# Moving small VectorE operations of a graph attention kernel to TensorE: own scores, both edge bounds and a constant one

## The reference

```python
h = x @ W                                      # 8192 x 128
e = (h @ a1)[:, None] + (h @ a2)[None, :]      # own score + neighbour's score
e = where(e > 0, e, 0.2 * e)                   # leaky slope
e = where(adj > 0, e, -9e15)
h_prime = softmax(e, axis=1) @ h
out = layernorm(x + elu(h_prime), eps=1e-5)    # over the 128 features
```

## Time and profile before

| what | us |
|---|---|
| median of 3 runs | 719.73 (718.51 to 720.04) |
| the profiled execution's own time | 722.26 |
| span of its profile | 720.5 |
| TensorE busy | 558.7 |
| VectorE busy | 482.4 |
| ScalarE busy | 520.8 |
| GpSimd busy | 440.6 |

### The profile page before, as it was taken

The page is one execution under the profiler, slowest core; times in us unless marked ns, Lnnn a source line. Parts: engine busy times, 40 slices in busy tenths (PEclk is TensorE's granted clock), DMA queues, the critical chain, the costliest instruction groups (busy, mean ns, idle before and its releaser), DMA issues.

```text
span 720.5 us, 11885 instructions
## 1 busy us (share of the span) xinstructions
PE 558.7 (78%) x3023; PEld 356.0 (49%) x3071; DVE 482.4 (67%) x2059; ACT 520.8 (72%) x414; POOL 440.6 (61%) x668
## 2 busy tenths in 40 slices
PE   0867887777777888787777988877777888787794
PEld 0333455444455555555445655554455555554483
DVE  1376677785766667777776567777766667776754
ACT  0847777777887878787887778787877878777410
POOL 2015457766766676767666576667766676776731
PEclk9978999997999988999998788999999988998955
DMA  8999999999999999999999999999999999999062
GB/s 351 328 417 429 425 421 428 428 423 425 427 428 426 427 428 426 425 429 425 427 429 426 428 425 428 426 429 428 425 425 430 428 426 428 425 426 407 24 171 80
DMA packets 34582, 285.57 MB, mean 396 GB/s; under 512 B 5512, under 2 KB 13856, under 8 KB 18048
## 3 DMA queue, kind: packets, MB, share of 16 engines
q1 hardware_dynamic: 29008, 276.83, 91.9%
q0 software_dynamic: 5120, 8.42, 3.3%
q10 hardware_dynamic: 432, 0.07, 0.1%
HBM read 283.18 MB, written 4.19 MB: 399 GB/s over the span
## 4 chain that ended last, share of the span: by engine, by line
DMA 71%; ACT 11%; PE 10%; issue 5%; DVE 2%; SPq 1%; ACTq 0%; POOLq 0%; POOL 0%; DVEq 0%
DMA adj_sb<-in_adj 68%; ACT adj_squared L558 10%; PE fold L660 5%; DMA a_sb<-in_L_gnn_a 2%; PE x_att_ps L713 1%; PE misc L685 1%; PE small L694 1%; PE fold L656 1%; SPq L402 1%; PE fold L757 1%; PE small L675 1%; PE x_att_ps L716 0%; DVE spread L376 0%; DVE stats L1000 0%; DVE x_sb L996 0%
## 5 line engine op out<-in xcount | busy, mean ns | idle before, releaser
L558 ACT ACTIVATE adj_squared<-adj_sb 128x4096 bf16<-128x4096 int32 x128 | 462.6, 3614 | 114.3 <-DMA adj_sb<-in_adj 111.7
L660 PE MATMUL fold<-adj_sb,bit_ident 128*128 128x512 bf16 x993 | 301.7, 448 | 9.1 <-DMA adj_sb<-in_adj 3.8
L503 POOL DMA_INDIRECT nb<-in_x,index x160 | 165.1, 1032 | 94.7 <-issue 68.7
L660 PEld LDWEIGHTS fold<-adj_sb,bit_ident 128*128 128x128 bf16 x1024 | 110.0, 107 | 151.6 <-issue 63.1
L868 DVE MAX8 top_map<-fold 128x8 f32<-128x512 f32 x128 | 89.5, 699 | 69.2 <-PE fold L660 64.3
L656 PE MATMUL fold<-col_no,ident_bf 128*128 128x512 bf16 x112 | 46.7, 417 | 111.3 <-DMA adj_sb<-in_adj 104.0
L364 POOL TENSOR_SCALAR edge_row<-row_iota,edge_in 128x128 f32<-128x128 int32 x186 | 128.1, 702 | 0.0
L382 POOL TENSOR_TENSOR spread<-edge_row,edge_w 128x384 f32<-128x384 f32 x60 | 54.4, 925 | 80.6 <-DVE edge_w L984 80.5
L656 PEld LDWEIGHTS fold<-col_no,ident_bf 128*128 128x128 bf16 x128 | 16.3, 127 | 131.8 <-issue 90.1
L483 POOL TENSOR_SCALAR empty_diag<-ident,counts 128x128 f32<-128x128 f32 x64 | 39.1, 616 | 59.6 <-DVE counts L904 32.7
L713 PEld LDWEIGHTS x_att_ps<-spread,nb 128*128 128x128 f32 x372 | 59.1, 226 | 9.2 <-issue 4.2
(11 more groups left out here) (120 smaller groups left out, 629.3 us busy)
## 6 DMA issues: line engine op xcount, KB each, us to landing
adj_sb<-in_adj SPq DMA_DIRECT2D x127, 2048.0 KB, 14.7
out<-x_sb SPq DMA_DIRECT2D x2, 1536.0 KB, 10.3
nb<-in_x,index POOLq DMA_INDIRECT x160, 2.4
adj_sb<-in_adj SPq DMA_DIRECT2D x2, 1024.0 KB, 16.1
out<-x_sb SPq DMA_DIRECT2D x5, 128.0 KB, 3.4
out<-x_sb SPq DMA_DIRECT2D x1, 384.0 KB, 10.0
W_sb<-in_L_gnn_W ACTq DMA_DIRECT2D x1, 64.0 KB, 7.8
x_sb<-in_x SPq DMA_DIRECT2D x4, 0.5 KB, 17.6
```

Source lines behind the costliest of these rows:

```text
L503: nc.gpsimd.indirect_dma_start(out=nb_of(j, g)[:, c, :], out_offset=None, in_=x[:, :], in_offset=bass.IndirectOffsetOnAxis(ap=index[:, g, ...
L558: nc.scalar.activation(adj_squared[:, h % 2, :], adj_sb[:, h % LOAD_SLOTS, :], ACT.Square, accum_out=half_sum[:, h:h + 1]).then_inc(square ...
L660: last = nc.tensor.matmul(fold[:, h % LOAD_SLOTS, :], bit_ident[:, b, :], adj_low[:, h % LOAD_SLOTS, b * FOLD:(b + 1) * FOLD, 0], start=Fa ...
```

## The change

TensorE makes four things that VectorE made, or makes them unneeded. A matmul with the identity puts the row's own score into `t_row_ps` ahead of the neighbours' scores (one matmul for each tile in `send_scores`). `count_starts` has a second matmul with a triangle that includes the diagonal, so it gives start and end of a row's edges at once, and `route` adds the base to both in one operation. `times_W` first adds a matmul of two rows of ones, so that PSUM holds h + 1; ScalarE takes off the one by a bias operand, and the minimum and the maximum of `finish` become one operation. `scores` takes the minimum with `cap` (whose low value is now NEG / ALPHA) ahead of the leaky slope. GpSimd keeps `found` and the ends by two copies in `tally` in place of one.

```diff
-        before = sb("before", [P, P], fp32)
+        before = sb("before", [P, 2, P], fp32)
-        starts_ps = misc[:, 160:160 + PAIR]
+        starts_ps = misc[:, 160:160 + 2 * PAIR].rearrange("p (t k) -> p t k", k=2)
...
-                    nc.gpsimd.tensor_copy(counts_all[:, :, tiles], counts[:]).then_inc(tallied, 1)
+                    nc.gpsimd.tensor_copy(found_all[:, tiles], found[:])
+                    nc.gpsimd.tensor_copy(ends_all[:, tiles], sent[:, :, END_COL]).then_inc(tallied, 1)
...
-                    nc.scalar.activation(z_exp[:, g, :, :], h_of(j, g)[:, :, 0:D], ACT.Exp).then_inc(elu_exp, 1)
+                    nc.scalar.activation(z_exp[:, g, :, :], h_of(j, g)[:, :, 0:D], ACT.Exp,
+                                         bias=minus_one[:, 0:1]).then_inc(elu_exp, 1)
...
-                    nc.tensor.matmul(starts_ps, before[:], found, start=True, stop=True).then_inc(starts_made, 1)
+                    for k in range(2):
+                        last = nc.tensor.matmul(starts_ps[:, :, k], before[:, k, :], found[:], start=True, stop=True)
+                    last.then_inc(starts_made, 1)
...
                     for t in range(PAIR):
+                        mine = s_all[:, bass.ds(j * BODY + g * PAIR + t, 1)]
+                        nc.tensor.matmul(t_row_ps[:, t, :], ident[:], mine.to_broadcast([P, SLOTS]),
+                                         start=True, stop=False)
                         for k, c in enumerate(SPANS[t]):
                             last = nc.tensor.matmul(t_row_ps[:, t, :], edge_row[:, g, t, k, :], t_slot[:, c, :],
-                                                    start=k == 0, stop=k == SPAN - 1)
+                                                    start=False, stop=k == SPAN - 1)
...
-                        last = nc.tensor.matmul(h_of(j, g)[:, t, 0:D], x_att[:, t, :], W_sb[:], start=True, stop=True)
+                        nc.tensor.matmul(h_of(j, g)[:, t, 0:D], ones[0:1, :], ones[0:1, :], start=True, stop=False)
+                        last = nc.tensor.matmul(h_of(j, g)[:, t, 0:D], x_att[:, t, :], W_sb[:], start=False, stop=True)
...
-                nc.vector.tensor_scalar(before[:], offset[:], 0.0, None, ALU.is_gt)
+                for k, compare in enumerate((ALU.is_gt, ALU.is_ge)):
+                    nc.vector.tensor_scalar(before[:, k, :], offset[:], 0.0, None, compare)
...
-                    v.after(nc.vector.tensor_tensor(sent[:, :, START_COL], starts_ps, tile_edge[:], ALU.add))
-                    v.after(nc.vector.tensor_tensor(ends, sent[:, :, START_COL], found, ALU.add))
+                    v.after(nc.vector.tensor_tensor(sent[:, :, START_COL:END_COL + 1], starts_ps,
+                                                    tile_edge[:].unsqueeze(2).to_broadcast([P, PAIR, 2]), ALU.add))
...
-                    v.after(nc.vector.tensor_tensor(score[:], t_row_ps, mine.unsqueeze(2).to_broadcast(slots),
-                                                    ALU.add))
-                    v.after(nc.vector.scalar_tensor_tensor(score_l[:], score[:], ALPHA, score[:],
-                                                           ALU.mult, ALU.max))
-                    v.after(nc.vector.tensor_tensor(score_l[:], score_l[:], cap[:, g, :, :], ALU.min))
+                    v.after(nc.vector.tensor_tensor(score[:], t_row_ps, cap[:, g, :, :], ALU.min))
+                    v.after(nc.vector.scalar_tensor_tensor(score_l[:], score[:], ALPHA, score[:], ALU.mult, ALU.max))
...
-                    v.after(nc.vector.tensor_scalar(z_one[:], z_exp[:, g, :, :], 1.0, None, ALU.min))
-                    nc.vector.scalar_tensor_tensor(elu[:], h_of(j, g)[:, :, 0:D], 1.0, z_one[:], ALU.add, ALU.max
+                    nc.vector.scalar_tensor_tensor(elu[:], z_exp[:, g, :, :], 1.0, h_of(j, g)[:, :, 0:D], ALU.min, ALU.max
```

More of the change, by code:

```diff
@@ L95, in graph_attention @@
     SENT = CODES + 2
-    ROW_COL, START_COL = CODES, CODES + 1
+    ROW_COL, START_COL, END_COL = CODES, CODES + 1, CODES + 2
     adj_tiles = adj.rearrange("(t p) c -> t p c", p=P)
@@ L155, in graph_attention @@
         is_code = sb("is_code", [P, PAIR, SLOTS], fp32)
-        counts = sb("counts", [P, 2, PAIR], fp32)
-        found, ends = counts[:, 0, :], counts[:, 1, :]
+        found = sb("found", [P, PAIR], fp32)
         below_end = sb("below_end", [P, PAIR, EDGES], fp32)
@@ L163, in graph_attention @@
         cap = sb("cap", [P, GROUPS, PAIR, SLOTS], fp32)
-        sent = sb("sent", [P, PAIR, SENT], fp32)
+        sent = sb("sent", [P, PAIR, SENT + 1], fp32)
         row_edge = sb("row_edge", [P, GROUPS, PAIR, EDGES], fp32)
@@ L190, in graph_attention @@
         empty_diag = sb("empty_diag", [P, GROUPS, PAIR, P], fp32)
-        z_one = sb("z_one", [P, PAIR, D], fp32)
         z_exp = sb("z_exp", [P, GROUPS, PAIR, D], fp32)
@@ L675, in fill_edges @@
                             last = nc.tensor.matmul(edge_in_ps[lo:hi, c, :], row_edge[:, g, t, e:e + hi - lo],
-                                                    sent[:, t, :], start=True, stop=True)
+                                                    sent[:, t, 0:SENT], start=True, stop=True)
                     last.then_inc(edges_filled, 1)
@@ L903, in lists @@
                     v.after(nc.vector.tensor_scalar(is_code[:], sent[:, :, 0:SLOTS], float(NO_CODE), None, ALU.is_gt))
-                    nc.vector.reduce_sum(found, is_code[:], AX.X).then_inc(listed, 1)
-                    nc.vector.tensor_scalar(cap[:, g, :, :], is_code[:], 1e30, NEG, ALU.mult, ALU.add)
+                    nc.vector.reduce_sum(found[:], is_code[:], AX.X).then_inc(listed, 1)
+                    nc.vector.tensor_scalar(cap[:, g, :, :], is_code[:], 1e30, NEG / ALPHA, ALU.mult, ALU.add)
                 def route(j, g):
@@ L910, in route @@
                     dve.wait_ge(starts_made, count(j, g))
-                    v.after(nc.vector.tensor_tensor(sent[:, :, START_COL], starts_ps, tile_edge[:], ALU.add))
-                    v.after(nc.vector.tensor_tensor(ends, sent[:, :, START_COL], found, ALU.add))
+                    v.after(nc.vector.tensor_tensor(sent[:, :, START_COL:END_COL + 1], starts_ps,
+                                                    tile_edge[:].unsqueeze(2).to_broadcast([P, PAIR, 2]), ALU.add))
                     for t in range(PAIR):
-                        last = nc.vector.tensor_scalar(below_end[:, t, :], edge_no[:, t, :], ends[:, t:t + 1], None,
+                        last = nc.vector.tensor_scalar(below_end[:, t, :], edge_no[:, t, :],
+                                                       sent[:, t, END_COL:END_COL + 1], None,
                                                        ALU.is_lt)
@@ L959, in scores @@
                     dve.wait_ge(t_sent, count(j, g))
-                    mine = s_all[:, bass.ds(j * BODY + g * PAIR, PAIR)]
-                    v.after(nc.vector.tensor_tensor(score[:], t_row_ps, mine.unsqueeze(2).to_broadcast(slots),
-                                                    ALU.add))
-                    v.after(nc.vector.scalar_tensor_tensor(score_l[:], score[:], ALPHA, score[:],
-                                                           ALU.mult, ALU.max))
-                    v.after(nc.vector.tensor_tensor(score_l[:], score_l[:], cap[:, g, :, :], ALU.min))
+                    v.after(nc.vector.tensor_tensor(score[:], t_row_ps, cap[:, g, :, :], ALU.min))
+                    v.after(nc.vector.scalar_tensor_tensor(score_l[:], score[:], ALPHA, score[:], ALU.mult, ALU.max))
                     v.after(nc.vector.reduce_max(row_max[:], score_l[:], AX.X))
```

## The result

The changed kernel took 722.98 us as the median of 13 runs, the kernel before 718.51 beside it: ratio 1.006, 95% interval 1.0041 to 1.008. It is slower, by 4.3 us going by the ratio (4.5 by the two medians), where 2.65 was forecast. The profiled execution of the changed kernel took 722.56, with a span of 720.7. One execution of a later kernel (own scores alone) took 770.2 us, at a mean granted clock of 0.63 over its whole span, and is left out of the comparisons.

A forecast was written before the change was run, and what follows sets the result against it. DMA loads of adj bound the kernel until about 666 us, then a chain alternating TensorE, mostly at low clock, with VectorE. 0.6 + 0.9 + 0.8 + 1.05 - 0.7 = +2.65 on 719.73 gave 722.4 us, range 719.4 to 724.8.

The forecast's parts named there:

- The stream: The adj loading until about 666 us: TensorE's added matmuls hide behind the DMA there, cost 0.
- Step 1: Last step's send_scores through times_W and count_starts to route: added records less VectorE's saved line 912, +0.6 us.
- Step 2: send_scores(back1): its 4 own-score records come after the wait for VectorE and count in full, +0.9 us.
- Step 3: times_W(back2): 0.9 to 1.05 us more, hidden by a 1.03 us TensorE pause behind it, cost 0.
- Step 4: send_scores(final): 4 more records at 2.37 / 12 us each, +0.8 us.
- Step 5: times_W(back1): twice 4 records more, counted in full because TensorE's own order is the bound, +1.05 us.
- the rival of the drain: One-row matmuls in times_W: 4 switches at 0.2 us each, 724.5 us; chance 0.11 including dearer records.
- Step 6: The last three finish lose line 990; the last maximum then waits for ScalarE's exponential, -0.7 us.
- one of the signs that the prediction named for itself being wrong: At the end, the granted clock between 684 and 709 us not being 0.50.
- the shares of the last group sent 3.35 us later: At the end, the changed kernel's profile would show the final group's send of shares 3.35 us later.
- The rival of the returning clock: At the end, TensorE returns to 2.4 GHz earlier, making the change faster: 712 to 718.2 us, chance 0.10.

The follow-up runs named there:

- the two filled kernels: Idle bf16 matmuls in three TensorE pauses at the end, added to the kernel before (0.9955) and to the changed kernel with 128-row products of ones (0.9939).
- ones_only: The kernel before with only the one-row products of ones in times_W, Exp's bias and the shorter finish; ratio 1.0018 to before.
- ones_first: The changed kernel with one 256-column one-row product for both tiles, then the two products with W; ratio 1.0047 to before.
- warm_after: The changed kernel, one-row products kept, with idle bf16 matmuls in three TensorE pauses at the end; ratio 1.0012 to before.
- own_only: The kernel before with only the own scores added by TensorE in send_scores, and cap ahead of the slope; ratio 1.0038 to before.
- ends_only: The kernel before with only the second triangle in count_starts, one operation fewer in route and two copies in tally; ratio 1.0004 to before.
- two_op_finish: The kernel before with finish as x + max(h, 0), then + min(exp(h), 1), nothing added to TensorE; ratio 1.0002 to before.
- ones_128_only: The kernel before with only the ones part, made as identity times a matrix of ones (128-row weights); ratio 0.9979 to before.
- ones_128_rows: The changed kernel with identity times a matrix of ones in place of one row times one row everywhere; 718.91 us, ratio 0.9988 to before.
- late_128: The changed kernel with 128-row products of ones only in the last four groups, one-row ones in the loop; 718.46 us, ratio 0.9991 to before.

## Why the prediction held, step by step

**The stream: right.** It cost nothing, as the unchanged DMA share, the least landing time and the end of the loads show, and as the version with one-row products in the loop alone confirms.

**Step 1, +0.6 forecast.** Between the two first profiles `below_end` moved from 678.36 to 679.42, +1.06. The chain shows why: `times_W` took 1.66 and not 0.88, so the 11 idle matmuls ended at 678.78, 1.6 later than the 677.20 of before. Line 912's operation and the second triangle come to nothing together, as forecast: the ends alone gave 1.0004.

**Step 2, +0.9: right.** 3.56 us for the 16 records of lines 687 and 690 (685.55 to 689.11) against 2.71. **Step 3, 0: right**, with a pause of 0.41 left in place of 1.03:

```profile
695.81 1.65 PE L718 MATMUL x_att_ps<-spread,nb 128*128 128x128 f32 x6 [0.41 <-DVE spread L374]
```

**Step 4, +0.8**, can't be read off, since the two profiles had different clocks there; at the high clock 16 records took 1.69 us (699.49 to 701.18), where 12 took 1.33. The prediction also gave VectorE's saved operation in `scores(final)` no value, which does not hold at the high clock (step 5).

**Step 5, +1.05: the term that was mis-sized.** The prediction gave the records of `times_W` the price of their neighbours. The runs showed two costs that the rival of the drain had only in half. First, each change between one-row and 128-row weights costs 0.19 us at 2.4 GHz (0.41 minus 0.22 per pair; with two changes a `times_W` takes 1.26, 0.38 over 0.88), 0.8 in a `times_W`. That rival's price, 0.2 a switch, was right, and its chance, 0.11 together with dearer records, too low. The argument against it, that mixed 128- and 64-column weights are no dearer, said nothing about rows. The page "TensorEngine Tiling (Array Packing)" of the Trainium skill, section Key Properties, says that a change of tiling mode drains the engine; the spacing agrees with it, if one row of weights is such a mode. Second, the clock falls afterwards. Around the idle matmuls that follow, all four profiles of kernels with one-row products at the end lose the high clock, in spite of an engine that is never idle (the two filled kernels without such products are left out; their TensorE was done by 705):

```
one-row products at the end     PEclk, 702 to 709 us
  changed kernel                0.55
  ones_only                     0.52
  ones_first                    0.58
  warm_after                    0.50
none at the end
  before, first profile         0.50 (low from 682 to 709)
  before, second profile        1.00
  own_only, ends_only           1.00, 1.00
  two_op_finish                 1.00
  ones_128_only, ones_128_rows  1.00, 1.00
  late_128                      1.00
```

The window is fixed in time and not in the program, but in the seven profiles with 1.00 the clock is up from 700 us until the shares of `final` are sent. One profile of each kernel can't tell how often this happens: three of the 12 runs of the filled changed kernel took 716.4 to 716.6 and may have escaped it.

Lower clock means 1.71 in place of about 0.86 for four idle matmuls and 1.95 in place of 1.28 for the shares, about 1.5 us. With 0.8 in step 1, 0.8 here and some in the last `times_W` that is 3 to 3.5 us for the ones, against 4 to 5 by the comparison of runs (0.72% between the changed kernel and the 128-row version). The remainder lies in executions that were not profiled and is open.

The prediction also said that this step has no cover. At the high clock before had some: in its second profile the chain goes from line 685 over `scores`, the Exp and `weights` of `final` (697.61 to 699.58, 1.97 us), and `times_W` with its idle matmuls runs beside that. With 128-row products TensorE is the bound, but hardly (700.87 to 702.77, 1.90 us); with one-row products it is so by far (701.18 to 704.60, 3.42 us).

**Step 6, -0.7: the size was right, the wait was not.** From the start of the last spread to the end of the last VectorE operation it was 10.43 us before (706.26 to 716.69) and 9.64 after (707.29 to 716.93), 0.79 less. The prediction had VectorE wait for ScalarE ahead of the last maximum. What it waits for is GpSimd, one operation earlier:

```profile
712.96 0.60 DVE L1018 TENSOR_SCALAR x_sb<-x_sb,mean_var,late_rstd 128x128 f32<-128x128 f32 x2 [0.99 <-POOL late_rstd L472]
713.04 0.47 ACT L568 ACTIVATE z_exp<-fold,minus_one 128x256 f32<-128x256 f32 x1 [1.82 <-PE fold L731]
...
713.54 0.42 DVE L994 SCALAR_TENSOR_TENSOR elu<-z_exp,fold 128x256 f32<-128x256 f32 x1
```

The maximum starts at 713.54, as line 1018 ends, without a wait of its own. The exponential ends at 713.51, so ScalarE would have been next by a hair. Up to the late scaling of `back1` (lines 1015 and 1018) the two `finish` that were to give 0.65 for certain gave 0.53 (6.20 us before, 5.67 after), because its factor queued behind GpSimd's factors of `back2`, whose `var_eps` took 0.48 and not 0.20; the other 0.26 came behind it. The bias operand costs 0.10 (0.47 against the 0.369 of the earlier trace rows), as estimated.

**What the forecast missed in its reading of before.** It took the clock of one execution for the kernel's: 0.50 from 683 to 709. The second profile had most of that stretch at 1.00. The changed kernel's own profile has 0.64 from 684 to 709, which is one of the signs that the prediction named for itself being wrong; another of its figures, the shares of the last group sent 3.35 us later, came to 1.03 between the two first profiles (703.57, 704.60) and 5.0 against the second (699.58). At the high clock TensorE's added records cost half, which should have made the loss smaller than 2.65; the one-row products made it larger. The sign was safe, the size came near by two errors that oppose each other, and that is luck. So is part of the nearness in absolute time (722.4 forecast, 722.98 measured): the forecast started from 719.73, 1.2 us above the 718.51 that before had beside the changed kernel. The rival of the returning clock, kept at 0.10 as a way to be faster, was the right question put to the wrong kernel: it was before that already had it.

**Open.** With one-row products the three parts add up to the whole (0.18%, 0.38% and 0.04%; 0.6% together). With 128-row ones they do not: own scores alone cost 0.38%, but beside 128-row ones they and the ends cost some 0.1% (0.9988 against 0.9979, up to 0.3% within the intervals). That the clock is granted differently is likely and was not shown. Nor is it shown why the clock falls behind one-row products. In the filled changed kernel the clock also fell once at 688.7, in a burst without one-row products, which the theory does not explain.

## What to carry to other kernels

When work moves to TensorE, the price of a matmul is that of its neighbours only if its weights have as many rows as theirs. Write a constant as identity times a matrix, and not as one row times one row, when it stands between 128-row products: it costs the same records. On a stretch where TensorE sets the order, read the granted clock in more than one execution before costing anything, because the runs of the same kernel lay up to 4.8 us apart, and in the two that were profiled the clock was the main difference. And fill the pauses first: here that was worth 0.45%, more than all four VectorE operations (0.12% at their best, within the noise).

## What the runs showed of the hardware that was not expected

- Two fp32 records with one row of weights between 128-row ones: 0.41 us at 2.4 GHz, against 0.22 for two with 128 rows, and the 128-row pair behind them 0.42 as well. Making the one-row side 256 columns wide, so that there are two changes and not four, saved 0.4 us of 1.66. At 1.2 GHz a pair took 0.72 (pairs of the filled changed kernel that start at 691.98, 692.70, 693.43 and 694.15), against 0.43 for two 128-row records of 128 columns (1.28 for six of line 718).
- The granted clock can fall to 1.2 GHz in a window in which TensorE is busy 7.00 of 7.00 us. The page "TensorE: Matmul & The Clock Gate" of the Trainium skill, Part 1, lets sustained activity release the throttle; busy time in the profile was not a measure of that activity here, neither for one-row products nor, in the first profile of before, for small fp32 ones.
- GpSimd's `var_eps` (128 x 2) took 0.48 us where it started together with a VectorE addition of two SBUF inputs (line 994 of the two-operation finish, line 999 of the changed kernel), and 0.20 where VectorE's operation read PSUM (both profiles of before).
- Filling three pauses with 18 bf16 products of 512 columns kept 2.4 GHz from 665 to 705 us in the profiled execution and moved the bound of that stretch from TensorE to VectorE.
